# Third layer of a four-layer kernel: where the routing remainder lies, who scales, when the first group is routed, and how rows become strips

## What is computed

```python
# layer 0: cond = per-image mix of 8 kernels (32x32 over the rows) + bias;  ffn = (silu(c Wg) * (c Wu)) Wd, 512 -> 1792 -> 512
# layer 1: cond = grouped convolution along the columns, 9 taps;           ffn = c Wbase + top-2 of 8 LoRA experts, rank 16
# layer 2 ("third layer"):
agg_w = einsum('bk,koi->boi', att, weight)             # att: softmax over 8 kernels, per image
c = einsum('boi,bih->boh', agg_w, x) + (att @ bias_k)[:, :, None]
logits = c @ router_weight.T + router_bias             # 64 experts, per row of 512
scores = softmax(logits); topk_w, topk_idx = top_k(scores, 8)
w_sum = topk_w.sum(-1); w_dense = scatter(topk_w, topk_idx)
x = x + c * w_sum + w_dense @ expert_bias
# layer 3: cond as in layer 0;  ffn = (c * in_scale) @ sign(W).T * out_scale + bias, scales from 8 softmax weights
```

## Time and profile before

| | |
|---|---|
| median of 3 runs | 539.9 us (539.55 to 539.94) |
| the profiled execution | 540.8 us, of it span 539.0 us |
| TensorE busy | 526.0 us (98%) |
| VectorE, ScalarE, GpSimd busy | 225.5, 147.5, 179.5 us |
| first layer (to about 356 us) | TensorE 351.8 of 356.0 us busy |
| second layer, 356 to 443.1 us | TensorE 86.9 of 87.1 us busy |
| third layer, 443.1 to 479.75 us | TensorE 31.6 of 36.7 us busy |
| fourth layer's products, 479.75 to 534.6 us | TensorE 54.7 of 54.9 us busy |

### The profile page before, as it was taken

One profiled execution on the slowest core, in us unless ns is written; L12 is line 12 of the kernel. 1 busy time (PEld: TensorE's weight loads), 2 busy tenths in 40 slices (PEclk: granted clock), 3 DMA queues, 4 the chain that ended last, 5 costly groups with the idle time before them and its releaser, 6 DMA issues.

```text
span 539.0 us, 7007 instructions
## 1 busy us (share of the span) xinstructions
PE 526.0 (98%) x2643; PEld 392.7 (73%) x2643; DVE 225.5 (42%) x518; ACT 147.5 (27%) x261; POOL 179.5 (33%) x171
## 2 busy tenths in 40 slices
PE   6999999999999999999999999999999997999997
PEld 6888888888888888888888886635353644567785
DVE  3532252622323622223623233635435226886665
ACT  4422222322222322222322222000002327556333
POOL 3299995400000400000300840040000205869656
PEclk9999999999999999999999999999999999999999
DMA  9299640196000230000204100969696946065973
GB/s 316 77 391 312 212 97 7 47 157 126 0 0 0 70 105 0 0 0 0 84 14 108 32 1 0 132 126 159 195 156 204 227 97 137 2 98 87 253 170 137
DMA packets 82087, 58.46 MB, mean 108 GB/s; under 512 B 61712, under 2 KB 66832, under 8 KB 81680
## 3 DMA queue, kind: packets, MB, share of 16 engines
q1 hardware_dynamic: 77712, 41.83, 35.8%
q0 software_dynamic: 4272, 16.25, 11.3%
q10 hardware_dynamic: 80, 0.08, 0.0%
HBM read 38.98 MB, written 12.81 MB: 96 GB/s over the span
## 4 chain that ended last, share of the span: by engine, by line
PE 93%; DVE 4%; issue 1%; DMA 1%; ACT 0%; POOL 0%; DVEq 0%; POOLq 0%
PE ps L724 91%; DVE wcat L1498 1%; DVE rest L1492 1%; PE ps L934 1%; DMA pack_a<-in_pack_a 1%; DVE m L1487 0%; PE ps L1058 0%; PE ps L892 0%; DVE tr L1360 0%; PE ps L956 0%; PE ps L950 0%; DVE xs L1305 0%; DVE ps L1305 0%; ACT osc L1148 0%; POOL silu L600 0%
## 5 line engine op out<-in xcount | busy, mean ns | idle before, releaser
L724 PE MATMUL ps<-c_hi,wl 128*128 128x512 f32 x448 | 169.9, 389 | 0.0
L724 PE MATMUL ps<-c_lo,wl 128*128 128x512 f32 x448 | 169.7, 389 | 0.0
L1305 DVE TENSOR_TENSOR hff<-silu,ps 128x512 f32<-128x512 f32 x56 | 38.5, 688 | 167.1 <-PE ps L724 167.1
L724 PEld LDWEIGHTS ps<-c_lo,wl 128*128 128x128 f32 x448 | 84.1, 188 | 17.4
L724 PEld LDWEIGHTS ps<-c_hi,wl 128*128 128x128 f32 x448 | 84.0, 188 | 17.4
L724 PE MATMUL ps<-wl,h_hi 128*128 128x512 f32 x224 | 87.6, 391 | 0.0
L724 PE MATMUL ps<-wl,h_lo 128*128 128x512 f32 x224 | 87.2, 389 | 0.0
L1182 ACT ACTIVATE silu<-ps 128x512 f32<-128x512 f32 x56 | 33.5, 598 | 118.5 <-PE ps L724 118.5
L1148 ACT ACTIVATE h_hi<-hff 128x512 fp32r<-128x512 f32 x56 | 35.4, 632 | 108.8 <-DVE hff L1305 108.8
L558 POOL TENSOR_TENSOR c_lo<-cT,c_hi 128x512 fp32r<-128x512 f32 x8 | 10.1, 1292 | 153.3 <-ACT c_hi L1148 153.3
L1305 DVE TENSOR_TENSOR h_lo<-hff,h_hi 128x512 fp32r<-128x512 f32 x56 | 44.4, 793 | 39.1 <-ACT h_hi L1148 39.1
(11 more groups left out here) (194 smaller groups left out, 590.0 us busy)
## 6 DMA issues: line engine op xcount, KB each, us to landing
wl<-in_wl POOLq DMA_DIRECT2D x14, 768.0 KB, 8.3
stg<-y_dram SPq DMA_DIRECT2D x64, 128.0 KB, 5.1
xs<-in_x SPq DMA_DIRECT2D x4, 1024.0 KB, 8.3
x_all<-in_x SPq DMA_DIRECT2D x1, 4096.0 KB, 14.3
y_dram<-prod SPq DMA_DIRECT2D x16, 256.0 KB, 2.2
x_all<-in_bias POOLq DMA_DIRECT2D x4, 1024.0 KB, 9.6
out_x<-x_all SPq DMA_DIRECT2D x15, 256.0 KB, 4.1
x_dram<-x_all SPq DMA_DIRECT2D x3, 1024.0 KB, 7.4
```

Source lines behind the costliest of these rows:

```text
L724: return pe.matmul(o, l, r, start=start, stop=stop)
L1305: return dve.tensor_tensor(o, a, b, op)
```

## The change

Five things, in one edit.

1. `rest` in route2 becomes `rest2`, in PSUM (bank 4, columns 0 to 255, where the logits lie before their turn and the turned weights after it). `ex` is in SBUF for all groups; for the last it was in bank 7.
2. The scaling of tiles 2 and 3 of `cS[g]` goes from GpSimd to VectorE (`scale_rows`). GpSimd only adds, and starts with its group's tiles.
3. `router2(0)`, `turn_logits2(0)`, `mix_rows(2)`, `turn_weights(0)`, `experts2(0, ...)` and `turn_c(1)` go into `last1`, among the products of tile 3 of the second layer; VectorE's residual of this tile comes after `route2(0)`. `layer2` runs for groups 1 and 2, with `turn_c(g + 1, (3,))` behind `turn_weights(g)`, and `experts2(g, 1)` is issued with the group after only from group 1 on. Banks of `mix_rows` and `turn_c` and the waits follow.
4. `spill` and `fetch` are gone, with `x_dram`. `restrip` makes 16 DMAs of 32 rows by 2 KB for a group, from `x_all` to `xT(g)` directly.
5. In the second layer's loop `turn_hm` comes before the convolutions, into bank 7, and only the last convolution waits for its copy. In `last2` chunks 2 and 3 of the fourth layer's condition change places: chunk 2 comes ahead of `router2(3)`, chunk 3 ahead of `turn_logits2(3)`, and VectorE's sums of both ahead of `route2(3)`.

The diff, cut to its core:

```diff
-        ex_last = bank(7)[:, 0:GT * E2].rearrange("p (j e) -> p j e", e=E2)
-
-        def ex_of(g):
-
-            return ex_last if g == G - 1 else ex[:]
+        rest2 = bank(4)[:, 0:GT * E2].rearrange("p (j e) -> p j e", e=E2)
 
...
 
         def rows_bank(g, j):
 
-            return bank(4 + j if g < 2 else (0, 5, 6, 7)[j])
+            return bank((4 if g < 2 else 2 if g == 2 else 0) if j == 0 else 4 + j)
...
         FIRST3 = (5, 6, 7, 5)
+
+        def turns(g):
+
+            return (2, 3, 0, 1) if g == 1 else range(GT)
...
 
-            def spill(g):
-
-                parts = ((0, GT, s_x_dram[g]),) if g < G - 1 else ((0, 2, s_x_dram[g]), (2, GT, s_x_dram_last))
-                for j0, j1, done in parts:
-                    sp.wait_ge(s_x_new[1], GT * g + j1)
-                    dst = x_dram[g * TOK + j0 * P:g * TOK + j1 * P].rearrange("(j p) n -> p j n", p=P)
-                    sp.dma_start(dst, x_all[:, g * GT + j0:g * GT + j1, :]).then_inc(done, 16)
-
-            def fetch(g):
-
-                sp.wait_ge(s_x_dram[g], 16)
+            def restrip(g):
+
                 if g == 0:
                     sp.wait_ge(s_cond_mm[1], G * Q)
                 if g == 2:
@@ -454,10 +442,10 @@
                 if g == G - 1:
                     sp.wait_ge(s_cond_mm[2], GT)
                 for j in range(GT):
-                    if g == G - 1 and j == 2:
-                        sp.wait_ge(s_x_dram_last, 16)
-                    src = x_dram[(g * GT + j) * P:(g * GT + j + 1) * P].rearrange("(b i) n -> i b n", b=TB)
-                    sp.dma_start(xT(g)[j * ROWS:(j + 1) * ROWS], src).then_inc(s_xT[g], 16)
+                    sp.wait_ge(s_x_new[1], GT * g + j + 1)
+                    for b in range(TB):
+                        sp.dma_start(xT(g)[j * ROWS:(j + 1) * ROWS, b],
+                                     x_all[b * ROWS:(b + 1) * ROWS, g * GT + j, :]).then_inc(s_xT[g], 16)
 
             sp.wait_ge(s_btab, 2)
             sp.dma_start(bias_dram, btab[:]).then_inc(s_bias_dram, 16)
...
             bias(1, 3)
-            spill(0)
-            spill(1)
-            fetch(0)
-            fetch(1)
-            spill(2)
-            fetch(2)
+            for g in range(G - 1):
+                restrip(g)
             bias(3, 0)
-            spill(3)
-            fetch(3)
+            restrip(G - 1)
             for g in range(1, G):
                 bias(3, g)
             for g in range(G):
...
             def add_rows(g):
-                pool.wait_ge(s_x_new[1], G * GT)
-                pool.wait_ge(s_share, g + 1)
-                pool.wait_ge(s_c_turned, GT * (g + 1))
-                for j in (2, 3):
-                    pool.tensor_scalar(cS[g][:, j], cS[g][:, j], share2[:, g, j:j + 1], None,
-                                       ALU.mult).then_inc(s_pool_scaled, 1)
+                pool.wait_ge(s_x_new[1], GT * (g + 1))
                 for j in (2, 3, 0, 1):
                     if j < 2:
                         pool.wait_ge(s_cS_scaled, 2 * g + j + 1)
                         pool.wait_ge(s_x_new[2], GT * g + j + 1)
                     else:
-                        pool.wait_ge(s_pool_scaled, 2 * g + j - 1)
+                        pool.wait_ge(s_cS_scaled_dve, 2 * g + j - 1)
                     xg = x_all[:, g * GT + j, :]
                     pool.tensor_tensor(xg, xg, cS[g][:, j], ALU.add).then_inc(s_c_added, 1)
 
...
             def layer1(g):
                 base(g, range(GT))
                 pe.wait_ge(s_hm, g + 1)
-                for q in range(Q - 1):
+                turn_hm(g, 7)
+                for q in range(Q):
+                    if q == Q - 1:
+                        pe.wait_ge(s_hmT, g + 1)
                     conv(g + 1, q)
-                pe.wait_ge(s_turned1, Q * (g + 1) + 1)
-                turn_hm(g, 4)
-                conv(g + 1, Q - 1)
                 lora_b(g)
                 lora_a_router(g + 1)
                 pe.wait_ge(s_x_new[1], GT * (g + 1))
 
             def mix_rows(g):
 
-                pe.wait_ge(s_xT[g], 16 * GT)
+                pe.wait_ge(s_xT[g], 16 * GT * TB)
                 if g == 1:
                     pe.wait_ge(s_cT[2], GT)
                 if g > 1:
+                    pe.wait_ge(s_cS, GT * g)
+                if g == 2:
+                    pe.wait_ge(s_x_new[1], GT * (G - 1) + 3)
+                if g > 2:
                     pe.wait_ge(s_cT[2], GT * (g - 1) + 1)
                 for j in range(GT):
                     at = slice(j * ROWS, (j + 1) * ROWS)
@@ -926,9 +908,15 @@
 
                 for j in js:
                     pe.wait_ge(s_cS, GT * g + j + 1)
-                    if g == 1:
-                        pe.wait_ge(s_x_new[1], GT * (G - 1) + j + 1)
-                    if g > 1 and j < 2:
+                    if g == 1 and j == 2:
+                        pe.wait_ge(s_cS, GT * (g + 1) + 1)
+                    if g == 1 and j == 3:
+                        pe.wait_ge(s_x_new[1], NT)
+                    if g == 1 and j < 2:
+                        pe.wait_ge(s_x_new[2], j + 1)
+                    if g == 2 and j >= 2:
+                        pe.wait_ge(s_x_new[2], j + 1)
+                    if g == 3 and j < 2:
                         pe.wait_ge(s_x_new[2], GT * (g - 2) + j + 1)
...
                 lora_b(g, (2,))
-                base(g, (3,))
+                pe.wait_ge(s_weights23, LOADS23)
+                router2(0)
+                base(g, (3,), (0,))
+                turn_logits2(0)
+                mix_rows(2)
+                base(g, (3,), (1, 2))
+                turn_weights(0)
+                base(g, (3,), (3,))
                 lora_b(g, (3,))
+                experts2(0, 0)
+                turn_c(1, turns(1))
+                pe.wait_ge(s_cT[2], GT + 2)
+                experts2(0, 1)
 
             def layer2(g):
-                if g == 0:
-                    pe.wait_ge(s_weights23, LOADS23)
                 router2(g)
                 turn_c(g + 1, (0,))
                 turn_logits2(g)
-                turn_c(g + 1, (1, 2, 3))
                 if g + 2 < G:
+                    turn_c(g + 1, (1, 2))
                     mix_rows(g + 2)
+                    turn_weights(g)
+                    turn_c(g + 1, (3,))
+                    pe.wait_ge(s_cT[2], GT * (g + 1) + 2)
+                    pe.wait_ge(s_cS, GT * (g + 2) + 1)
                 else:
+                    turn_c(g + 1, (1, 2, 3))
                     x_ready(0)
                     pe.wait_ge(s_blk[3], 1)
                     for s in (0, 1):
                         cond_chunk(3, 0, s, FIRST3[s])
-                turn_weights(g)
-                pe.wait_ge(s_cT[2], GT * (g + 2))
-                if g:
+                    turn_weights(g)
+                    pe.wait_ge(s_cT[2], GT * (g + 2))
                     experts2(g - 1, 1)
-                if g + 2 < G:
-                    pe.wait_ge(s_cS, GT * (g + 2) + 1)
                 experts2(g, 0)
 
             def last2(g):
+                cond_chunk(3, 0, 2, FIRST3[2])
                 router2(g)
-                cond_chunk(3, 0, 2, FIRST3[2])
-                turn_logits2(g)
                 pe.wait_ge(s_cT[3], 1)
                 cond_chunk(3, 0, 3, FIRST3[3])
+                turn_logits2(g)
                 pe.wait_ge(s_x_new[2], GT * (g - 1))
                 experts2(g - 1, 1)
                 router3(0)
                 turn_weights(g)
                 turn_logits3(0)
-                pe.wait_ge(s_share, G)
                 pe.wait_ge(s_x_new[2], GT * (g - 1) + 2)
                 experts2(g, 0)
...
                 layer1(g)
             last1(G - 1)
-            for g in range(G - 1):
+            for g in range(1, G - 1):
...
                 for j in js:
-                    act.wait_ge(s_c_turned, GT * g + j + 1)
+                    act.wait_ge(s_c_turned, GT * g + turns(g).index(j) + 1)
...
                 act.wait_ge(s_wcat_turned, g + 1)
-                copy(wT2[g % 2][:], bank(4)[:, 0:2 * P]).then_inc(s_wT2, 1)
+                copy(wT2[(g + 1) % 2][:], bank(4)[:, 0:2 * P]).then_inc(s_wT2, 1)
 
             def layer2(g):
                 logits_out(g)
                 store_c(g + 1, (0, 1))
                 exp(s_shifted2, s_exp2, g, E2)
-                store_c(g + 1, (2, 3))
                 if g + 2 < G:
+                    store_c(g + 1, (2,))
                     rows_out(g + 2, (0,))
-                weights_out(g)
-                if g + 2 < G:
+                    weights_out(g)
+                    store_c(g + 1, (3,))
                     rows_out(g + 2, (1, 2, 3))
+                else:
+                    store_c(g + 1, (2, 3))
+                    weights_out(g)
                 scale_rows(g, (0, 1))
 
             act.wait_ge(s_biasN, 1)
             rows_out(0)
             store_c(0)
             rows_out(1)
-            for g in range(G - 1):
+            logits_out(0)
+            exp(s_shifted2, s_exp2, 0, E2)
```

(55 more changed lines are left out.)

19 lines of the change are left out of this document (8 added, 11 removed).

## The result

Slower, by 0.7%: the changed kernel takes 543.69 us in the median (543.41 to 544.52), the kernel before, run beside it, 540.17 us (539.55 to 540.83). The ratio is 1.0066, with a 95% interval of 1.0053 to 1.0079, so the difference is small but clear of the noise. The forecast was 537.2 us, its range 535.9 to 539.6; what came is its second rival, the late strips, which it had at 541.7 us, and 2 us on top of that.

A forecast was written before the change was run, and what follows sets the result against it. TensorE, busy 98%, was taken as the bound, with 5.05 us idle in the third layer to win from. 0.87 + 1.15 + 0.98 - 0.35 = 2.65, say 2.7; 539.9 - 2.7 = 537.2 us, range 535.9 to 539.6.

The forecast's parts named there:

- second rival: On SP's queue, strips come late at 0.61 us an issue; mix_rows(2) waits 4.5 us: 541.7 us, chance 0.10.
- Rows re-laid in SBUF: On SP's queue, 48 issues at 0.43 us land with margins 2.0, 5.9 and 4.2 us: cost nothing.
- the hold and its cures: VectorE's wcat waits for GpSimd's adds, 1.65 us in group 1, 1.40 in group 2; remainder in PSUM and moved scaling end it.
- the scaling on VectorE: On VectorE, between 0.17 and 0.68 us each; taken as 0.68, not held by GpSimd's add.
- rival 1: One VectorE scaling of each pair waits 1.24 us for a GpSimd add: 539.0 us; chance 0.20 with similar partial losses.
- early routing: First group's routing inside the second layer, TensorE's work the same in number: its 0.87 us of idle is gained.
- four weight turns: Sign of being right: TensorE's wait there none in groups 0 and 2, 0.8 us in group 1, about 1.2 in the last.
- VectorE busy without a gap: Sign of being right: VectorE works without pause ahead of the last group's weight turn, where TensorE waits about 1.2 us.
- covers of 0.0 to 0.1 us: Ahead of turn_c(1), tile 3's residual and final2 were to arrive just before TensorE asks, 0.0 to 0.1 us to spare.
- the last group's 0.35: In the last group VectorE becomes the bound; its chain lets the weight turn come 2.65 us earlier, losing 0.35 of 3.0.
- the loop: Second layer's loop with turn_hm before the convolutions: nothing either way, at worst 3 x 0.1 us.
- a mix_rows that waits for a DMA: Sign of being wrong: TensorE's mix_rows held up by strips not yet landed; no size given.

The follow-up runs named there:

- the first experiment: The changed kernel with the strips of groups 0 to 2 through DRAM again, only group 3 re-laid inside SBUF: 537.58 us, ratio 0.9947.

## Why the prediction was wrong

**The failed step: "Rows re-laid in SBUF. Cost nothing."** Its sum was 48 x 0.43 us against covers of 2.0, 5.9 and 4.2 us. The issue's time was taken from `fetch` (0.43 us), a transfer with a different source, and the measured pace was 0.63 us. With that, the step's own formula gives 414.0 + 48 x 0.63 + 3.0 = 447.2 for the last strip. The issues began 1.9 us earlier, the strip landed 1.0 us quicker, and over all 48 the pace was 0.65; it came at 444.64. With `fetch`'s own 0.46 us from issue to issue, instead of the length of one, the forecast's sum would still have been in time. The step weighed the new issues as bytes: it bounded them by 152 GB/s and explained the 0.61 us of `regroup`, the only row that spoke against it, by its 128 KB. The kernels with twice the issues and with two queues show that between 32 and 64 KB an issue the bytes do not set it. The price of an operation without a row had bounds of 0.43 and 0.61 us; the upper one would have cost the whole gain, and it was given 0.10.

**What stood behind the wait was in no term.** Rival 2 had the wait right, 4.5 us against 4.19, but not the clock. A wait of this length on TensorE made the next 2.89 us of work last 5.01. 537.2 + 4.2 + 2.1 = 543.5 us, against 543.69 measured; as said at the first experiment, that the 537.2 fits so well is in part luck. The 2.1 is the profiled execution's: the six of this kernel have granted clocks of 0.993 to 0.997, without the times following them, and the kernel with five unused products, 2.0 us faster in the median, is what bears the term out. The section "Part 1: The HAM clock gate" of the Trainium skill's page "TensorE: Matmul & The Clock Gate" has this as a block that halves the array's clock when TensorE has been idle; by that rule, the trace agrees: 0.58 and 0.50 behind the two waits of over 4 us, and 1.00 with unused products in their place.

**Right: the hold and its cures.** The 1.65 + 1.40 us of the two held groups came out as 1.65 in the first (1.95 to 0.30 or 0.31) and all of the wait in the second; the stretch lost 2.8 us, of which 0.2 is the end of the running products, which a wait exposes and a gapless follow-on hides (16 products ahead of group 2's weight turn take 1.95 us to their end, and 1.78 to the next start in the kernel with the remainder in PSUM, which has no wait there). The step took both cures as one; the runs show that each is enough. That the hold would pass on to `share` was not foreseen.

**Right: the scaling on VectorE.** It takes 0.48 us, between the bounds of 0.17 and 0.68, and none of the six was held (rival 1). The prediction's estimate from the Trainium skill was 0.33 us; the measured 0.48, and 0.40 from one start to the next, lie between it and the row that was taken. Of its rule on the shared read interface this shows little: only the end of a second scaling ever ran beside an add.

**Right in the waits, wrong in the sum: early routing.** Forecast for the four weight turns: none, 0.8, none, 1.2 us, then 0.46 for the copy; measured none, 0.74, none, 0.99, 0.46. The wait in the last group has another cause than "VectorE busy without a gap": VectorE stands idle for TensorE's last chunk of the fourth layer's condition, whose sum now comes ahead of route2(3):

```profile
476.35 0.69 DVE L1313 TENSOR_TENSOR xs<-ps,bias_bc 128x512 f32<-128x512 f32 x1 [0.72 <-PE ps L702]
```

Not foreseen were 0.29 us at turn_logits(2), for ScalarE's copy `lgT` (it stood behind the two scalings before as well, but `store_c` of the last turned tile, 0.60 us, is new ahead of them), and the work: "TensorE's work is the same in number" was true (300 products), but the same products took 0.50 us more. Two places are seen in the first experiment's kernel. The 16 turns of turn_c(1) take 2.21 us to the next instruction, where they took 2.04 in two parts. That is not the price of 16 turns in a row, for those of turn_c(0), also in one go, take 1.75 in the kernel before; it is where the covers of 0.0 to 0.1 us were forecast, and single turns start up to 0.2 us late there, which the timeline does not show as idle. And base(3) takes 3.64 in three parts where it took 3.43 in one. Together that is 0.38 us of the 0.50. In the forecast's own terms the early routing was worth 0.87 less the 0.49 of a piece of cover taken from group 1, and with the last group's 0.35 next to nothing. Measured, it is 0.75 us worse together with the new order in `last2` than both left out; which share is whose stays open.

**Right: the loop.** Nothing was forecast, "at worst 3 x 0.1 us", and at most 0.3 us is there; the one wait that came with it, 0.20 us, is of the kind that was feared.

The prediction's list of what would show it wrong began with "a mix_rows that waits for a DMA", and it was that. What failed was not the reading of the layer but the price of one issue, 48 times over in one queue.

## What to carry to other kernels

When a change turns few large transfers into many small ones, sum the issues on their queue first, with the slowest row of that queue and not with that of the most similar transfer, and compare the end of the sum with when the data is wanted; bytes per second come second. A wait of some microseconds on the engine that is the bound costs more than its length when the clock falls behind it, so a rival that has such a wait needs a term for the work after it. Where one small instruction is held by another engine, move one operand or one piece of work, see which instruction is held next, and time each cure alone: here the smallest edit had the whole gain, and the rest of the change gave it back.
